# The last expert's rows by blocks, the projections' weights loaded a stage earlier, and their first quad by tiles

## The chip, the cores and the metric

The program runs on one core of one Trainium2 chip. Its time is in device microseconds, the median of several executions. The core has TensorE (PE, with its weight loads as PEld), VectorE (DVE), ScalarE (ACT), GpSimd (POOL), SyncE (SP), which here only issues transfers and waits, and 16 DMA engines that all queues share.

## The reference

Three stages on x of shape 2 x 2048 x 256 (4096 tokens):

```
x = x + 0.5 * ffn(layernorm(x))      # stage 1
x = x + attention(layernorm(x))      # stage 2
x = x + 0.5 * ffn(layernorm(x))      # stage 3, the same weights as stage 1
```

`ffn` is a shared gated network (gelu(x Wsg) * (x Wsu), times Wsd, hidden width 512) plus 16 experts of the same form. Each expert takes the 256 tokens of each of the 2 batches with the highest gate scores, and its rows, times the gate's weight, are added into the output at their tokens (a scatter with addition). `attention` is causal, 16 heads of 16, with rotary positions on queries and keys, and a projection at the end.

## The kernel before

**Blocks.** The program is a row of blocks: constants, `ffn` (stage 1, from line 241, its block opens at L251), `projections` (L1009, block L1019), `exact_shift` (a guarded block that is skipped with these inputs), `attention` (L1444, block L1459), and `ffn` again. Inside a block each engine runs its own instruction list, and semaphores tie the lists together. A block ends for all engines at once: each engine's queue executes a DRAIN, they report to one another, and the next block begins on all of them. The last wait of any engine's list therefore holds the start of the next block.

**Products.** Each float32 product is made of three passes over split operands (`product3`, L168 to L172: high x high, high x low, low x high).

**Experts.** `ffn` works on items of 512 rows: 8 of the shared network, then 16 experts. For an item, TensorE makes the gate and up products (`gu`), ACT and DVE make the hidden rows and their split (`hidden`, `mul`, `low`), TensorE makes the down product (`down`: 4 blocks q of 128 rows, each over 4 chunks c of the hidden width, 3 passes, so 48 matmuls), DVE multiplies it by the gate's weight on the way out of PSUM (`evacuate`, L863, two blocks q after each half h), and GpSimd issues one indirect DMA with addition for each block q (`scatter`, L976). For the last item (`last` in `down`) the chunks that don't need the last hidden rows come first, for q = 0 and 2; then comes the rest of q = 0 and the whole of q = 1, after which `s_D` is signalled for half 0, and then the other half. `scatter` waits for `s_ev`, which DVE signals after both blocks of a half. `pD` holds the four results in two PSUM banks; `pX` and `pC` are two more banks, in which gathered rows are turned, and they are free at that point. At the end GpSimd waits until all scatters have landed:

```
                for k in range(2):
                    s_sc[k].wait(g, E // 2)
```

SyncE loads the experts' weights (`load_weight`, L496). The last one is that of expert 15, after which its list is empty.

**Projections.** This block reads stage 1's result in 8 quads of 4 tiles (512 tokens), in a rotation of 3 buffers `xq`. SyncE issues, in this order: quad 0, `WqkT` (512 KB), `WvT` (256 KB), quad 1, the bias, the rotary table `trig` (2 MB in one), quad 2, and a zero fill of the `shift` rows. For a quad, DVE computes the statistics (L1216, L1223) and the scale, ACT the deviation (L1150) and the normalized rows `xn` (L1156, four instructions, one for each tile), TensorE turns them (L1096, 8 transposes), ACT copies the turned columns (`columns`, L1164), DVE makes their low part (`low_columns`, L1237), and then TensorE makes four row products (`rows`) and `values`. DVE rotates (L1247), GpSimd adds the parts (L1302, L1303, L1307), and SyncE stores the halves (`store`, L1066). From quad 4 on, SyncE also loads heads for the attention (`load_head`, L1435).

The projections' weights are split in this block. ACT's list begins so:

```
                deviation(0)
                a.wait_ge(*s_w.at(2))
                s_wh.done(a.activation(w[0][:, :, :], raw[:, :, :], ACT.Copy))
                normalize(0)
                deviation(1)
                normalize(1)
                columns(0)
```

GpSimd's begins with three small memsets; then it waits for that copy, computes the low part (L1295, a subtraction of 128 x 1536), and sets `sk` (L1296). `rows` waits for this low part (`s_wl`) and for `s_xl`.

## Time and profile before

| what | us |
|---|---|
| runs of the kernel before | 1663.20, 1664.07, 1666.24; median 1664.07 |
| the profiled execution's own time | 1666.25 |
| its span, from the first to the last instruction | 1664.5 |
| time outside the span | 1.75 |

The blocks of the profiled execution, from the span's start: `ffn` up to 499.3, `projections` from 499.33, `attention` from 629.07, the second `ffn` from 1167.78 to the end at 1664.5. Times in the profile are measured from the span's start. In the timeline a row is: start, duration, engine, line, operation, written<-read, shape, count, and in brackets how long the engine sat idle before it and what released it. "POOLq" or "PEq" is that engine's instruction queue, which does waits and drains without being busy. The granted clock of TensorE is 1.0 at 2.4 GHz and 0.5 at 1.2 GHz.

### The profile page before, as it was taken

The page shows a single profiled execution, that of the slowest core. Times are in us where ns is not written, and L with a number is a line of the kernel's source. Part 1 is how long each engine was busy: PE and PEld are TensorE (multiplying, and loading weights), DVE is VectorE, ACT ScalarE, POOL GpSimd, SP SyncE. Part 2 cuts the span into 40 slices and gives each one's busy share as a digit, 9 for nine tenths or more (in the row PEclk, how much of TensorE's full clock was granted, in tenths as well). Part 3 has the DMA queues.
Part 4 walks back from the last instruction along what each step waited for, and adds up shares of the span by engine and source line. Part 5 has one row for each costly group of instructions (what it writes and reads, how often), then busy time and mean ns, then how long its engine had stood idle before and what let it go on. Part 6 is the DMA issues. An engine that isn't in the chain of part 4 may idle for free. (4 is left out here: it accounts for less than half of the span.)

```text
span 1664.5 us, 26482 instructions
## 1 busy us (share of the span) xinstructions
PE 1516.9 (91%) x9945; PEld 1054.1 (63%) x9945; DVE 861.7 (52%) x1848; ACT 995.6 (60%) x1359; POOL 563.2 (34%) x496
## 2 busy tenths in 40 slices
PE   4999999999966867999999999998599999999996
PEld 3788888988955652333333333333478888898895
DVE  6887676766736650032022122122688767676673
ACT  7322255445415757989999999997732225544541
POOL 3000356566445772111121111110300035656644
PEclk9999999999987987999999999999699999999999
DMA  7221256666534799225044343100722126666753
GB/s 274 70 89 51 75 161 152 153 156 152 116 38 168 218 220 198 38 41 77 7 74 80 100 79 65 14 14 29 274 70 89 51 75 161 153 153 155 155 114 38
DMA packets 120752, 183.14 MB, mean 110 GB/s; under 512 B 19568, under 2 KB 83056, under 8 KB 117360
## 3 DMA queue, kind: packets, MB, share of 16 engines
q1 hardware_dynamic: 91440, 130.04, 30.7%
q0 software_dynamic: 29184, 51.40, 14.8%
q8 instruction: 79, 1.29, 0.3%
q14 instruction: 49, 0.40, 0.1%
HBM read 125.82 MB, written 55.57 MB: 109 GB/s over the span
## 5 line engine op out<-in xcount | busy, mean ns | idle before, releaser
L1710 ACT ACTIVATE 8019_pr<-8019_pS 128x1024 f32<-128x1024 f32 x448 | 421.3, 1073 | 17.3 <-PE 8019_pS L1631 16.2
L1661 PE MATMUL 8019_pO<-8019_pr,6201_vres 128*32 128x512 f32 x1792 | 240.2, 608 | 4.5 <-DVE 8019_tO L1735 3.6
L1631 PEld LDWEIGHTS 8019_pS<-sq_rows,sk_rows 50*128 50x128 f32 x896 | 74.9, 186 | 216.9 <-ACT 8019_pr L1710 157.5
L1631 PE MATMUL 8019_pS<-sq_rows,sk_rows 50*128 50x512 f32 x896 | 186.3, 468 | 25.2 <-DMA sq_rows<-shift 20.8
L1735 DVE STREAM_TRANSPOSE 8019_tO<-8019_pO 128x512 f32<-128x512 f32 (+1 forms) x33 | 23.0, 699 | 313.8 <-PE 8019_pO L1661 313.8
L170 PE MATMUL 14694_pGU<-columns_XT,weights_wts 128*128 128x512 f32 x384 | 152.5, 397 | 1.6 <-DVE columns_XT L844 1.6
L170 PE MATMUL 110_pGU<-columns_XT,weights_wts 128*128 128x512 f32 x384 | 152.5, 397 | 1.6 <-DVE columns_XT L844 1.6
L1724 POOL TENSOR_SCALAR_AFFINE_SELECT 8019_pr<-8019_pr 128x512 f32<-128x512 f32 x32 | 21.5, 673 | 381.0 <-ACT 8019_pr L1710 381.0
L171 PE MATMUL 14694_pGU<-columns_XT,weights_wts 128*128 128x512 f32 x384 | 149.8, 390 | 0.0
L171 PE MATMUL 110_pGU<-columns_XT,weights_wts 128*128 128x512 f32 x384 | 149.8, 390 | 0.0
L172 PE MATMUL 110_pGU<-columns_XT,weights_wts 128*128 128x512 f32 x384 | 149.7, 390 | 0.0
L172 PE MATMUL 14694_pGU<-columns_XT,weights_wts 128*128 128x512 f32 x384 | 149.7, 390 | 0.0
L709 ACT ACTIVATE hidden_hT<-110_hf 128x512 fp32r<-128x512 f32 x96 | 60.7, 632 | 144.7 <-DVE 110_hf L834 143.1
L709 ACT ACTIVATE hidden_hT<-14694_hf 128x512 fp32r<-128x512 f32 x96 | 60.7, 632 | 144.3 <-DVE 14694_hf L834 142.8
L976 POOL DMA_INDIRECT out<-14694_eo,14694_idx x64 | 109.6, 1712 | 100.3 <-issue 66.9
L976 POOL DMA_INDIRECT x_after_ffn<-110_eo,110_idx x64 | 109.5, 1711 | 99.9 <-issue 66.6
L170 PE MATMUL 14694_pD<-weights_wts,hidden_hT 128*128 128x256 f32 x384 | 111.0, 289 | 1.4 <-DVE hidden_hT L839 1.4
L170 PE MATMUL 110_pD<-weights_wts,hidden_hT 128*128 128x256 f32 x384 | 111.0, 289 | 1.4 <-DVE hidden_hT L839 1.4
L172 PE MATMUL 110_pD<-weights_wts,hidden_hT 128*128 128x256 f32 x384 | 108.6, 283 | 0.0
L172 PE MATMUL 14694_pD<-weights_wts,hidden_hT 128*128 128x256 f32 x384 | 108.6, 283 | 0.0
L171 PE MATMUL 110_pD<-weights_wts,hidden_hT 128*128 128x256 f32 x384 | 108.5, 283 | 0.0
L171 PE MATMUL 14694_pD<-weights_wts,hidden_hT 128*128 128x256 f32 x384 | 108.5, 283 | 0.0
(318 smaller groups left out, 3334.4 us busy)
## 6 DMA issues: line engine op xcount, KB each, us to landing
token_table<-weights_xn POOLq DMA_DIRECT2D x16, 512.0 KB, 6.3
110_raw_g<-WgT SPq DMA_DIRECT2D x16, 512.0 KB
110_raw_u<-WuT SPq DMA_DIRECT2D x16, 512.0 KB
110_raw_d<-WdT SPq DMA_DIRECT2D x16, 512.0 KB
q_rows<-rows_half SPq DMA_DIRECT2D x32, 256.0 KB, 3.4
k_rows<-rows_half SPq DMA_DIRECT2D x32, 256.0 KB, 3.3
sq_rows<-q_rows SPq DMA_DIRECT2D x32, 256.0 KB
sk_rows<-k_rows SPq DMA_DIRECT2D x32, 256.0 KB
```

Of the source, the lines that this page charges most:

```text
L170: pe.matmul(out, w_hi, x_hi, start=start, stop=False)
L171: pe.matmul(out, w_hi, x_lo, start=False, stop=False)
L172: return pe.matmul(out, w_lo, x_hi, start=False, stop=stop)
L709: s_hh.done(a.activation(hT[0][:, i % 2, f, :], hf[:, f % 2, :], ACT.Copy))
L976: s_sc[k].part(g.indirect_dma_start(out, bass.IndirectOffsetOnAxis(rows_[:, q:q + 1], 0), eo[:, k, q, :], None, compute_op=ALU.add), 16)
L1631: m = t_.matmul(to[:, e, :], key, query, start=True, stop=True)
L1661: m = t_.matmul(pO[e * 32:(e + 1) * 32, off:off + wd], vres[:, (g // GB) * TPB + kt, at:at + 32], from_(e), start=n == first[j], stop=n == ...
L1710: s_exp.done(a.activation(to, pS[:, u % RING, :, :], ACT.Exp, scale=HD ** -0.5))
L1724: s_mask.done(g.affine_select(out=blk_, in_=blk_, compare_op=ALU.is_ge, fill=0.0, base=0, pattern=[[0, GH], [1, P]], channel_multiplier=-1))
L1735: s_copy.done(v.transpose(tO[:, part], pO[:, part]))
```

## The change

- **The last expert, in both `ffn` blocks.** Each block q of the down product gets a PSUM bank of its own (`own_bank`: two halves of `pD`, `pX` and `pC`). The early chunks are those of q = 0 and 1. After each block's last chunk TensorE signals `s_Dq`; DVE evacuates that block alone and signals `s_evq`; GpSimd scatters it after that signal.
- **The wait for the scatters' landing** moves from the end of GpSimd's list to the end of SyncE's.
- **Loads of the projections' weights** move into the first `ffn` block: SyncE issues both behind the last expert's weights, into a buffer at a fixed address (`qkv_raw`) that nothing else uses in that block.
- **Splitting these weights**: the high part moves from ACT (Copy) to GpSimd (`tensor_copy`), behind its three small memsets and in front of the subtraction.
- **The first quad** is loaded by four DMAs of one tile (128 KB), each with its own semaphore. DVE's statistics start tile by tile; ACT signals each normalized tile (`s_n0`), and TensorE turns tile by tile. ACT now does `columns(0)` ahead of `normalize(1)`.
- **The rotary table** is loaded in four parts of 512 KB, with quads 1 and 2 ahead of parts 0 and 1; SyncE's order is: four tiles, bias, quad 1, part 0, quad 2, parts 1, 2, 3, zero fill.

```diff
+            s_Dq, s_evq = sig("pe_last_D"), sig("dve_last_ev")
+            own_bank = lambda q: (pD[:, 0, 0, :], pX[:, 0:D], pD[:, 1, 0, :], pC[:, 0:D])[q]
...
+                if following:
+                    following(sp)
+                for k in range(2):
+                    s_sc[k].wait(sp, E // 2)
...
+                def rows_down(d, q, c, to):
+                    k = slot(d)
+                    rows_ = slice(q * P, (q + 1) * P)
+                    return self.product3(t_, to, hT[0][:, d % 2, c, rows_], hT[1][:, d % 2, c, rows_],
+                                         weight(k, 2, 0)[:, c, :], weight(k, 2, 1)[:, c, :], c == 0, c == FC - 1)
...
-                    s_ev.wait(t_, 2 * (d - 1) + (2 if last else h + 1))
-                    order = [(q, c) for q in (2 * h, 2 * h + 1) for c in range(FC) if (q, c) not in early]
-                    if h == 0:
-                        order = early + order
-                    for q, c in order:
-                        if last and (q, c) == (0, FC - 1):
-                            t_.wait_ge(*s_hl.at(4 * (d + 1)))
...
+                def last_down(d):
+                    t_.wait_ge(*s_hl.at(4 * d + FC - 1))
+                    s_wl.wait(t_, 3 * (d - J) + 3)
+                    s_ev.wait(t_, 2 * d)
+                    for q in range(2):
+                        for c in range(FC - 1):
+                            rows_down(d, q, c, own_bank(q))
+                    t_.wait_ge(*s_hl.at(4 * (d + 1)))
+                    for q in range(4):
+                        for c in range(FC - 1 if q < 2 else 0, FC):
+                            m = rows_down(d, q, c, own_bank(q))
+                        s_Dq.done(m)
...
+                    if s > NI:
+                        last_down(NI - 1)
+                    elif s > J + 1:
...
+                def evacuate_last(d):
+                    k = d % 2
+                    s_sc[k].wait(v, (d - J) // 2)
+                    s_wt.wait(v, d - J + 1)
+                    for q in range(4):
+                        v.wait_ge(*s_Dq.at(q + 1))
+                        s_evq.done(v.tensor_scalar(eo[:, k, q, :], own_bank(q), wt[:, k, q:q + 1], 0.5,
+                                                   ALU.mult, ALU.mult))
...
-                        if q % 2 == 0:
+                        if item == NI - 1:
+                            g.wait_ge(*s_evq.at(q + 1))
+                            self.settle(g)
+                        elif q % 2 == 0:
                             g.wait_ge(*s_ev.at(2 * item + q // 2 + 1))
                             self.settle(g)
...
                         scatter(s - 2)
-                for k in range(2):
-                    s_sc[k].wait(g, E // 2)
...
-                load(0)
-                s_w.done(sp.dma_start(raw[:, :, 0:2 * D], self.ins["WqkT"].rearrange("(c p) f -> p c f", p=P)))
-                s_w.done(sp.dma_start(raw[:, :, 2 * D:], self.ins["WvT"].rearrange("(c p) f -> p c f", p=P)))
-                load(1)
+                for j in range(4):
+                    s_x0[j].done(sp.dma_start(xq[:, 0, j, :], xv[0][:, j, :]))
                 s_c.done(sp.dma_start(bias[:, :], self.ins["b_rows"]))
-                s_c.done(sp.dma_start(trig[:, :, :], self.ins["c_rope"]))
-                load(2)
+                for k in range(S // W):
+                    if k < 2:
+                        load(k + 1)
+                    part = slice(k * W, (k + 1) * W)
+                    s_trig[k].done(sp.dma_start(trig[:, :, part], self.ins["c_rope"][:, :, part]))
                 sp.wait_ge(*s_clear.at(1))
                 s_zero.done(sp.dma_start(self.shift.rearrange("h c (k s) -> h (c k) s", s=512),
                                          zero[:, :].unsqueeze(1).to_broadcast([B * H, 2 * S // 512, 512])))
...
-                turn(0)
+                for j in range(4):
+                    t_.wait_ge(*(s_n0.at(j + 1) if j < 3 else s_xn.at(1)))
+                    for c in range(DC):
+                        m = t_.transpose(pX[:, c, j * P:(j + 1) * P], xn[:, 0, j, c * P:(c + 1) * P], self.ident[:, :])
+                        if j == 3:
+                            s_T.done(m)
...
+                        if q == 0 and j < 3:
+                            s_n0.done(m)
                     s_xn.done(m)
...
                 deviation(0)
-                a.wait_ge(*s_w.at(2))
-                s_wh.done(a.activation(w[0][:, :, :], raw[:, :, :], ACT.Copy))
                 normalize(0)
                 deviation(1)
+                columns(0)
                 normalize(1)
-                columns(0)
...
-                    s_x[q % 3].wait(v, q // 3 + 1)
+                    if q > 0:
+                        s_x[q % 3].wait(v, q // 3 + (q % 3 > 0))
                     s_mv.wait(v, q - 1)
                     for j in range(4):
+                        if q == 0:
+                            v.wait_ge(*s_x0[j].at(1))
                         m = v.bn_stats(st6[:, q % 2, j, :], xq[:, q % 3, j, :])
...
-                    v.wait_ge(*s_c.at(2))
+                    v.wait_ge(*s_c.at(1))
+                    if n < 4 * (S // W):
+                        v.wait_ge(*s_trig[q].at(1))
...
+                g.wait_ge(*s_w.at(0))
+                s_wh.done(g.tensor_copy(w[0][:, :, :], raw[:, :, :]))
                 g.wait_ge(*s_wh.at(1))
                 s_wl.done(g.tensor_tensor(w[1][:, :, :], raw[:, :, :], w[0][:, :, :].bitcast(f32), ALU.subtract))
                 s_clear.done(g.memset(self.sk[:, 0, :, :].bitcast(f32), 1.0))
...
+    def load_projection_weights(self, sp):
+
+        s_w = self.counter("proj_w", 16)
+        s_w.done(sp.dma_start(self.qkv_raw[:, :, 0:2 * D], self.ins["WqkT"].rearrange("(c p) f -> p c f", p=P)))
+        s_w.done(sp.dma_start(self.qkv_raw[:, :, 2 * D:], self.ins["WvT"].rearrange("(c p) f -> p c f", p=P)))
...
-        prog.ffn(ins["x"], prog.x1, first=EARLY)
+        prog.ffn(ins["x"], prog.x1, first=EARLY, following=prog.load_projection_weights)
```

## Rows read from the trace of the kernel before

**Rows 1.** The page, part 1: busy time and share of the span of each engine.
```profile
PE 1516.9 (91%) x9945; PEld 1054.1 (63%) x9945; DVE 861.7 (52%) x1848; ACT 995.6 (60%) x1359; POOL 563.2 (34%) x496
```

**Rows 2.** Windows: stretch, length, busy time by engine, granted clock, DMA share, GB/s.
```profile
499.30:520.00 20.70, 7.19 (x21) 5.60 (x22) 8.28 (x26) 8.94 (x15) 8.75 (x5) 0.50 0.74 266
595.00:615.50 20.50, 16.00 (x96) 12.87 (x94) 12.44 (x21) 11.66 (x21) 18.98 (x12) 1.00 1.01 189
```

**Rows 3.** Timeline of the end of the second ffn: down product, evacuation, scatter.
```profile
1645.43 0.38 PE L170 MATMUL 14694_pD<-weights_wts,hidden_hT 128*128 128x256 f32 x1 [1.44 <-DVE hidden_hT L839]
...
1649.78 0.88 DVE L863 TENSOR_SCALAR 14694_eo<-14694_pD,14694_wt 128x256 f32<-128x256 f32 x2 [3.62 <-PE 14694_pD L172]
...
1651.44 1.55 POOL L976 DMA_INDIRECT out<-14694_eo,14694_idx  x1 [6.85 <-DVE 14694_eo L863]
...
1657.02 1.56 POOL L976 DMA_INDIRECT out<-14694_eo,14694_idx  x1 [0.30 <-issue]
```

**Rows 4.** Timeline of the first ffn's end, POOL alone.
```profile
491.86 1.55 POOL L976 DMA_INDIRECT x_after_ffn<-110_eo,110_idx  x1 [0.30 <-issue]
499.33 0.52 POOL L1290 MEMSET 6206_zero<- 32x512 f32 x1 [5.92 <-POOLq L251]
```

**Rows 5.** Queue instructions by line: count, duration ns min/median/max, first and last start.
```profile
L59 POOLq EVENT_SEMAPHORE  x1: 17/17/17, 495.7 to 495.7; - x1
L251 POOLq DRAIN  x2: 3168/3170/3172, 495.9 to 1661.1; - x2
```

**Rows 6.** Attention's end, where SyncE has the last wait: store, its landing, next load.
```profile
1163.43 0.36 SPq L1574 DMA_DIRECT2D x_after_attn<-rows_acc  x1
1167.78 0.36 SPq L492 DMA_DIRECT2D hidden_xq<-x_after_attn  x1
...
x_after_attn<-rows_acc SPq DMA_DIRECT2D x1, 512.0 KB, 3.9
```

**Rows 7.** Timeline of the projections' first 21 us.
```profile
500.26 0.94 POOL L1293 MEMSET 6201_vres<- 128x512 f32 x1
500.80 0.47 SPq L1057 DMA_DIRECT2D 6206_xq<-x_after_ffn  x1
503.09 1.41 DVE L1216 BATCH_NORM_STATS2 6206_st<-6206_xq 128x6 f32<-128x256 f32 x4 [3.29 <-DMA 6206_xq<-x_after_ffn]
505.60 0.16 DVE L1231 SCALAR_TENSOR_TENSOR 6206_shift<-6206_mv,6206_rstd 128x4 f32<-128x4 f32 x1
505.75 1.48 ACT L1188 ACTIVATE 6206_w<-6206_raw 128x1536 fp32r<-128x1536 f32 x1 [0.40 <-DMA 6206_raw<-WvT]
507.10 1.41 DVE L1216 BATCH_NORM_STATS2 6206_st<-6206_xq 128x6 f32<-128x256 f32 x4 [1.34 <-DMA 6206_xq<-x_after_ffn]
507.14 2.06 ACT L1156 ACTIVATE 6206_xn<-6206_xq,6206_shift,6206_rstd 128x256 f32<-128x256 f32 x4
507.32 3.43 POOL L1295 TENSOR_TENSOR 6206_w<-6206_raw,6206_w 128x1536 fp32r<-128x1536 f32 x1 [6.11 <-ACT 6206_w L1188]
509.10 0.28 ACT L1150 ACTIVATE 6206_std<-6206_mv,49_eps 128x4 f32<-128x4 f32 x1
509.25 1.97 PE L1096 MATMUL 6206_pX<-49_ident,6206_xn 128*128 128x128 f32 x8 [22.96 <-ACT 6206_xn L1156]
512.78 1.05 ACT L1164 ACTIVATE sk_xT<-6206_pX 128x512 fp32r<-128x512 f32 x2
514.78 0.77 PE L170 MATMUL 6206_pQ<-sk_xT,6206_w 128*128 128x512 f32 x1 [3.56 <-issue]
519.99 1.03 PE L1096 MATMUL 6206_pX<-49_ident,6206_xn 128*128 128x128 f32 x8
```

**Rows 8.** Landing of SyncE's stores of 256 KB (L1066), us from issue: min, median, max.
```profile
DMA to landing us min/median/max: 2.8/3.4/13.3
```

**Rows 9.** SyncE's last load before the change's new ones.
```profile
441.62 0.37 SPq L496 DMA_DIRECT2D 110_raw_d<-WdT  x1
```

**Rows 10.** Timeline of the projections' end.
```profile
620.70 1.06 ACT L1175 ACTIVATE rows_half<-sq_turns 128x1024 fp32r<-128x1024 f32 x1 [9.10 <-DMA q_rows<-rows_half]
```

More of the change, by code:

```diff
@@ L28 @@
 EARLY = 2
+QKV_AT = 216 * 1024
 NBITS = 30
@@ L197, in load_constants @@
         self.x_at = at
+        self.qkv_raw = nc.alloc_sbuf_tensor_at("qkv_raw", [P, DC, 3 * D], self.f32, offset=QKV_AT)
         with self.scope() as t, nc.Block() as blk:
@@ L238, in _, with ffn @@
                 dve.wait_ge(s_cast, 3)
-    def ffn(self, x, out, first=0):
+    def ffn(self, x, out, first=0, following=None):
         nc, ALU, ACT, AX, bass = self.nc, self.ALU, self.ACT, self.AX, self.bass
@@ L938, in _ @@
                         split(s, 1)
-                    if s > J + 1:
+                    if s > NI:
+                        evacuate_last(NI - 1)
+                    elif s > J + 1:
                         evacuate(s, 0)
```

32 lines of the change are left out of this document (16 added, 16 removed).

## Prediction

> **What bounds the kernel now.** The page shows TensorE busy for 91% of the span [rows 1], so most of the kernel is TensorE's pace, and this change leaves that work as it is. It acts in three places where TensorE stands still. The windows show two of them around the projections: in their first 21 us TensorE is busy for 7.2 us at granted clock 0.50, which is its 1.2 GHz level, and from 595 on the DMA engines are full, at share 1.01 [rows 2]. The timeline of an `ffn` block's end shows the third: the last down product starts at 1645.43, the first scatter at 1651.44, and scatters follow 1.86 us apart ((1657.02 - 1651.44) / 3) until 1658.58 [rows 3]. After that nothing is computed until the span's end at 1664.5. The first `ffn` block ends in the same way: last scatter done at 493.41, next block at 499.33 [rows 4]. The queue view names what fills those 5.92 us: the landing is seen at 495.7, and then GpSimd's DRAIN runs from 495.9 for 3.17 us, the same length in both blocks, on an idle engine [rows 5].
>
> **Part 1: the last rows by blocks.** Before, DVE's first evacuation waits for 33 of the 48 matmuls, and the first scatter for two evacuations. From the first matmul to DVE's start are 4.35 us for the 33 [rows 3], 0.13 each at most; the tail behind the last one is in it, so I take 0.12. Afterwards block 0 is complete after 21 matmuls (18 early, 3 more): 12 fewer, 1.4 us. Its evacuation alone takes about 0.44 of the pair's 0.88: 0.4 us. The first scatter starts **1.8 us earlier**, near 1649.6. Later blocks are ready in time: each comes 12 matmuls (1.4 us) after the one before, and the scatters are 1.86 apart. Of that spacing 0.30 is issue [rows 3], also where a wait stands in between, so I count nothing for two more waits on GpSimd. The matmuls are the same 48. The early ones (18 x 0.12 = 2.2 us, as many as now) cover the wait for the last hidden rows as before.
>
> **Part 2: who awaits the landing.** Once GpSimd doesn't wait, its DRAIN can start right behind the last scatter, say 0.1 us, instead of 2.5 us (493.41 to 495.9 [rows 4, 5]). If its 3.17 us is a fixed length, it ends 3.3 us behind the scatter. SyncE sees the landing 2.3 us behind it (495.7 - 493.41) and ends the block faster: the attention block's last store, issued at 1163.43, lands 3.9 us later at 1167.3, and the next block's load starts at 1167.78 [rows 6], 0.45 us later. So SyncE would be ready at 2.8 us, and the drain decides. From the drain's end to the next block took 0.26 us (495.92 + 3.17 = 499.09 to 499.33 [rows 4, 5]). Scatter to next block is then 0.1 + 3.17 + 0.25 = 3.5 us instead of 5.92: **2.4 us**. The trace doesn't show this drain with transfers in flight. Its bounds: if it starts to count only at the landing, the gain is about 0.2 us; if it is nearly free behind the scatter, SyncE decides and the gain is 3.1. I take the fixed length, since both blocks show 3.17 within 4 ns [rows 5]. Each `ffn` block's end is worth 1.8 + 2.4 = 4.2 us, twice: **8.4 us**. Queued behind SyncE's new wait is nothing but the block's end. Ahead of it stand the two new weight loads.
>
> **Part 3: the projections' first quad** (times from the block's start at 499.33). Now row products start at 514.78, so at 15.45 [rows 7]. The chain: quad 0 lands at 3.75, statistics until 5.17, scale and shift until 6.43; then ACT copies the weights (505.75 to 507.23), normalizes, waits for quad 1's shift, normalizes that, and only at 512.78 copies quad 0's columns [rows 7].
>
> Afterwards:
> - *Tiles.* Four issues instead of one. The fourth goes out at the place that 500.80 had: 1.47 [rows 7]. A landing takes 2.8 us at the least, for 256 KB [rows 8], and 3.7 for the present quad (503.09 - 499.33 [rows 7]). I take 2.8, the nearer in size: it lands at 4.3, its statistics (one of four, 0.4) end at 4.7 against 5.17. The bounds are +0.4 and -0.5 us.
> - *ACT.* From statistics to shift 1.26 us (504.50 to 505.76 [rows 7]), and no copy behind it: 6.0. Four tiles 2.06: 8.1. TensorE turns three of them meanwhile and the last in 0.5 (a quarter of 1.97, plus a start): 8.65.
> - *Quad 1.* ACT's next deviation needs its statistics. Its DMA is sixth in SyncE's queue, so issued at about 2.5, landed at 6.2 (3.7 us); from landing to deviation are 2.0 us (507.10 to 509.10) and 0.28 for it [rows 7]: 8.5. That is just hidden behind the turns. If it took 6.3 us, as it did behind the weights (500.80 to 507.10 [rows 7]), columns would start at 11.1.
> - *Columns to products.* 512.78 to 514.78 is 2.0 us [rows 7]: products at 10.75.
> - *GpSimd's copy* isn't in the trace. Nearest are ACT's 1.48 us for the same tile and GpSimd's subtraction, 3.43 with two inputs [rows 7]. It starts at 1.87 (501.20). Copy and subtraction end at 6.8 to 8.75. The products need them at 10.75, so 2 us cover even the upper bound; I take 2.3 for it. Without the cover it would cost what it overruns.
>
> **Gain 15.45 - 10.75 = 4.7 us**, bounds 2.3 (late quad 1) and 5.1. The table's parts: part 0 is behind 1 MB, needed at about 13; the old 2 MB in one came behind 1.75 MB and held nobody.
>
> The Trainium skill speaks against four small loads: "DMA: Bandwidth & Descriptors", section "Anatomy of one DMA — SWDGE (gpsimd) path", gives each DMA about 2.0 us fixed and then the bytes at 436 GB/s. By this, for a path that isn't SyncE's, a quad is an estimated 3.2 us and a tile 2.3; the last tile would land at 3.8 and gain about 0.5 us rather than my 0.4, if the fixed parts overlap. The trace has 3.75 for the quad, so it is a little slower than the rule.
>
> **Does the 4.7 us last?** The window at 595 has GpSimd busy 18.98 of 20.5 us and the DMA engines at 1.01 [rows 2], and ACT waits 9.10 us for a store's landing [rows 10]. A DMA-bound tail can swallow a head start. But all these transfers are issued by SyncE behind stores that wait for GpSimd, so the queue begins to fill earlier too. I count the whole.
>
> **Part 4: the moved loads.** 768 KB go out behind 441.62 [rows 9], 58 us before they are needed, with no expert left to load. The last expert's own transfer is ahead in the same queue. At the rate of 266 GB/s that the projections' start shows [rows 2] they are 3 us of traffic beside scatters, for whose landing only the next item's scatters wait. The first blocks' items go on at TensorE's pace; I cost it at nothing. Without that cover it would be those 3 us.
>
> **The clock.** TensorE starts the quad at the low level either way: eight transposes take 1.97 us then and 1.03 when the clock is up [rows 7]. It was up at 519.99, 5.2 us after the products began [rows 7]. A shifted start may meet an earlier or later rise: plus or minus 1 us.
>
> **Sum.** 8.4 + 4.7 = 13.1 us. Of the profiled execution's 1666.25 us (span 1664.5 and 1.75 outside) that leaves 1653.1. This execution was 2.2 us above the median, so from 1664.07: **1651.0 us**.
>
> **Rivals.**
> - *The drain follows the landing.* GpSimd's drain may need its transfers finished before its 3.17 us begin. For it: in both blocks it came right behind the landing, so the trace can't separate the two. Against: no reason in its constant length. Each end loses 2.2 us: 1651.0 + 4.4 = 1655.4.
> - *The head start is lost in part.* Quad 1 comes late (1653.4), or the DMA-bound tail takes all of it (1655.7). For: [rows 2, 10]. Against: the queue's order.
> - *Both together*: 1658 to 1660.
> - *The loads' fixed costs add up* instead of overlapping: about 5.5 us later for the last tile, no gain in the projections, 1655.7. Against: stores issued 0.6 us apart landed in 2.8 us each at best [rows 8].
> - *The change does little*: its waits are only renamed, within 3 us of before. Part 1's 1.8 us twice already speak against it.
> - *Slower: the clock stays down in the projections.* The quad's work by tiles leaves TensorE's starts more scattered. Low clock makes its work take about twice as long [rows 7], so each us at it costs about 0.5 us of work. It would eat the 13 us only from 26 us more at the low level on; 40 us more would give 1651 + 20 = 1671. Against: it was up after 5.2 us, and at 1.00 in the busy window at 595 [rows 2].
>
> **Chances.** Forecast 0.58 (its own range 1648.5 to 1653); drain follows landing 0.17; head start lost in part or whole, for any of the three causes, 0.15; both 0.05; does little 0.03; slower by the clock 0.02. The range runs from 1648, for a cheap drain (0.7 us at each end) and a good rise of the clock, to 1656.5, for either single loss; that leaves out about 0.15. A measurement of this kernel tells 0.2% (3.3 us) from no change. Faster by more than that: 0.95; within it 0.03; slower 0.02.
>
> **What would show it.** Right: the last expert's first scatter 4.2 us behind its first down product instead of 6.0; GpSimd's drain right behind the last scatter, 3.2 us long; next block 3.5 us behind the scatter; projections' products 10.5 to 11 us into their block, with quad 1 landed by 6.5; attention's start as much earlier as these. Wrong: a drain of 5 us or more; a second idle stretch of ACT ahead of the columns; products waiting for GpSimd's copy; stores at the projections' end landing at the old times.

## The result and the profile after

| | before | after |
|---|---|---|
| median of 5 runs, us | 1664.69 (1663.20 to 1666.24) | 1655.38 (1650.51 to 1656.72) |
| the profiled execution, us | 1666.25, span 1664.5 | 1650.51, span 1648.7 |

The ratio is 0.9923, 95% interval 0.9903 to 0.9942, so 9.7 to 16.1 us less; the medians alone are 9.3 us apart. A second measurement of the same kernel (below) gave 0.9914, 0.9887 to 0.9942. The forecast of 13.1 us less lies inside both intervals. The median of 1655.38 is inside the forecast's range, but 4.4 above its 1651.0 and at the numbers of two rivals, 1655.4 and 1655.7; the second measurement's 1652.41 is not. So the times alone don't choose between them, and the traces have to. The profiled execution is 15.7 us shorter, and its blocks say where. Worked out from the first instruction of each block:

| us | before | after | gain |
|---|---|---|---|
| first `ffn`, from the span's start | 499.34 | 495.27 | 4.07 |
| projections with the skipped block | 129.74 | 121.93 | 7.81 |
| of that, up to the first row product | 15.44 | 11.41 | 4.03 |
| attention | 538.70 | 538.58 | 0.12 |
| second `ffn`, to the span's end | 496.76 | 492.88 | 3.88 |

Page, part 1, and windows of the kernel after, as in [rows 1, 2] (the windows are moved with the block):

```profile
PE 1508.1 (91%) x9943; PEld 1047.6 (64%) x9945; DVE 862.7 (52%) x1848; ACT 994.2 (60%) x1358; POOL 564.2 (34%) x497
```

```profile
495.27:516.00 20.73, 11.48 (x53) 9.13 (x54) 12.85 (x38) 9.52 (x18) 12.60 (x8) 0.65 0.70 229
591.00:611.50 20.50, 8.67 (x51) 6.63 (x51) 7.77 (x14) 8.34 (x16) 15.57 (x10) 0.85 1.06 260
```

In the first 21 us of the projections TensorE is busy for 11.5 us instead of 7.2, and for part of them at the high clock. The second window is later in the block's work than [rows 2] shows, since the block is ahead; the DMA engines are as full.

Timeline of the end of the second `ffn`, kernel after, PE, DVE and POOL, as in [rows 3]:

```profile
1633.81 0.38 PE L171 MATMUL 14727_pD<-weights_wts,hidden_hT 128*128 128x256 f32 x1 [1.44 <-DVE hidden_hT L859]
...
1636.72 0.48 DVE L892 TENSOR_SCALAR 14727_eo<-14727_pD,14727_wt 128x256 f32<-128x256 f32 x1 [2.18 <-PE 14727_pD L173]
...
1637.99 1.55 POOL L1010 DMA_INDIRECT out<-14727_eo,14727_idx  x1 [5.02 <-DVE 14727_eo L892]
...
1643.57 1.56 POOL L1010 DMA_INDIRECT out<-14727_eo,14727_idx  x1 [0.30 <-issue]
```

The first scatter starts 4.18 us behind the last down product's start, before 6.01. The scatters stand 1.86 apart as before, with 0.30 of issue between them: each block's rows are there in time.

Queue instructions of that line, kernel after (durations in ns, first and last start), and POOL's next instruction, as in [rows 4, 5]:

```profile
L253 POOLq DRAIN  x2: 7515/7524/7532, 487.5 to 1640.9; - x2
```

```profile
490.15 1.55 POOL L1010 DMA_INDIRECT x_after_ffn<-111_eo,111_idx  x1 [0.30 <-issue]
495.27 0.51 POOL L1336 MEMSET 6213_zero<- 32x512 f32 x1 [3.57 <-POOLq L253]
```

The DRAIN now enters the queue while the scatters run, so its 7.5 us are mostly their time. It ends at 495.02, 3.32 us behind the last scatter (491.70) and 1.03 us behind the landing (493.99), and the next block begins at 495.27: 3.57 us instead of 5.92.

Timeline of the projections' start, kernel after, as in [rows 7]:

```profile
497.01 1.45 POOL L1341 CAST 6213_w<-qkv_raw 128x1536 fp32r<-128x1536 f32 x1
497.30 1.97 DVE L1260 BATCH_NORM_STATS2 6213_st<-6213_xq 128x6 f32<-128x256 f32 x4 [1.56 <-DMA 6213_xq<-x_after_ffn]
498.55 3.41 POOL L1343 TENSOR_TENSOR 6213_w<-qkv_raw,6213_w 128x1536 fp32r<-128x1536 f32 x1
500.37 1.62 DVE L1275 SCALAR_TENSOR_TENSOR 6213_shift<-6213_mv,6213_rstd 128x4 f32<-128x4 f32 x1
501.91 1.39 DVE L1260 BATCH_NORM_STATS2 6213_st<-6213_xq 128x6 f32<-128x256 f32 x4
502.02 2.07 ACT L1197 ACTIVATE 6213_xn<-6213_xq,6213_shift,6213_rstd 128x256 f32<-128x256 f32 x4 [1.90 <-DVE 6213_shift L1275]
504.00 0.28 ACT L1191 ACTIVATE 6213_std<-6213_mv,49_eps 128x4 f32<-128x4 f32 x1
504.53 0.16 DVE L1275 SCALAR_TENSOR_TENSOR 6213_shift<-6213_mv,6213_rstd 128x4 f32<-128x4 f32 x1
504.66 1.09 ACT L1207 ACTIVATE sk_xT<-6213_pX 128x512 fp32r<-128x512 f32 x2 [0.38 <-PE 6213_pX L1168]
506.68 0.77 PE L171 MATMUL 6213_pQ<-sk_xT,6213_w 128*128 128x512 f32 x1 [1.84 <-issue]
510.90 1.03 PE L1132 MATMUL 6213_pX<-49_ident,6213_xn 128*128 128x128 f32 x8
```

The row to look at is 500.37: DVE's shift of 128 x 4 elements takes 1.62 us. The same instruction on the next quad takes 0.16. It ends at 501.99, and GpSimd's subtraction ends at 501.96. The kernel before has it too, and the prediction passed over it: its second shift started under the same subtraction (507.32 to 510.75 in [rows 7]) and lasted until 510.77:

```profile
509.63 1.14 DVE L1231 SCALAR_TENSOR_TENSOR 6206_shift<-6206_mv,6206_rstd 128x4 f32<-128x4 f32 x1
```

### The profile page after: what moved, and what is told of

The parts are those of the page before. It is cut to its first block and busy times, and to the rows that moved or that the text cites. A ratio compares the mean times of both kernels' runs of the same rounds, so it can differ in the third digit from the quotient of the medians.

```text
span 1648.7 us, 26498 instructions
## 1 busy us (share of the span) xinstructions
PE 1508.1 (91%) x9943; PEld 1047.6 (64%) x9945; DVE 862.7 (52%) x1848; ACT 994.2 (60%) x1358; POOL 564.2 (34%) x497
## 3 DMA queue, kind: packets, MB, share of 16 engines
q8 instruction: 79, 1.29, 0.3%
## 5 line engine op out<-in xcount | busy, mean ns | idle before, releaser
L1764 ACT ACTIVATE 8052_pr<-8052_pS 128x1024 f32<-128x1024 f32 x448 | 421.2, 1073 | 17.2 <-PE 8052_pS L1685 15.9
L1715 PE MATMUL 8052_pO<-8052_pr,6208_vres 128*32 128x512 f32 x1792 | 240.3, 606 | 5.9 <-DVE 8052_tO L1789 3.7
L1685 PEld LDWEIGHTS 8052_pS<-sq_rows,sk_rows 50*128 50x128 f32 x896 | 74.5, 185 | 213.9 <-ACT 8052_pr L1764 153.8
L1685 PE MATMUL 8052_pS<-sq_rows,sk_rows 50*128 50x512 f32 x896 | 185.3, 466 | 24.1 <-DMA sq_rows<-shift 19.6
L171 PE MATMUL 111_pGU<-columns_XT,weights_wts 128*128 128x512 f32 x384 | 152.5, 397 | 1.6 <-DVE columns_XT L864 1.6
L171 PE MATMUL 14727_pGU<-columns_XT,weights_wts 128*128 128x512 f32 x384 | 152.5, 397 | 1.6 <-DVE columns_XT L864 1.6
L172 PE MATMUL 14727_pGU<-columns_XT,weights_wts 128*128 128x512 f32 x384 | 149.8, 390 | 0.0
L172 PE MATMUL 111_pGU<-columns_XT,weights_wts 128*128 128x512 f32 x384 | 149.8, 390 | 0.0
L173 PE MATMUL 111_pGU<-columns_XT,weights_wts 128*128 128x512 f32 x384 | 149.8, 390 | 0.0
L173 PE MATMUL 14727_pGU<-columns_XT,weights_wts 128*128 128x512 f32 x384 | 149.8, 390 | 0.0
L1010 POOL DMA_INDIRECT out<-14727_eo,14727_idx x64 | 109.6, 1712 | 98.5 <-issue 67.0
L1010 POOL DMA_INDIRECT x_after_ffn<-111_eo,111_idx x64 | 109.5, 1711 | 98.1 <-issue 66.6
L171 PE MATMUL 111_pD<-weights_wts,hidden_hT 128*128 128x256 f32 x376 | 108.7, 289 | 1.4 <-DVE hidden_hT L859 1.4
L171 PE MATMUL 14727_pD<-weights_wts,hidden_hT 128*128 128x256 f32 x376 | 108.7, 289 | 1.4 <-DVE hidden_hT L859 1.4
L173 PE MATMUL 14727_pD<-weights_wts,hidden_hT 128*128 128x256 f32 x376 | 106.3, 283 | 0.0
L173 PE MATMUL 111_pD<-weights_wts,hidden_hT 128*128 128x256 f32 x376 | 106.3, 283 | 0.0
L172 PE MATMUL 14727_pD<-weights_wts,hidden_hT 128*128 128x256 f32 x376 | 106.2, 283 | 0.0
L172 PE MATMUL 111_pD<-weights_wts,hidden_hT 128*128 128x256 f32 x376 | 106.2, 283 | 0.0
```

The costliest lines, as they stand in the source:

```text
L171: pe.matmul(out, w_hi, x_hi, start=start, stop=False)
L172: pe.matmul(out, w_hi, x_lo, start=False, stop=False)
L173: return pe.matmul(out, w_lo, x_hi, start=False, stop=stop)
L1010: s_sc[k].part(g.indirect_dma_start(out, bass.IndirectOffsetOnAxis(rows_[:, q:q + 1], 0), eo[:, k, q, :], None, compute_op=ALU.add), 16)
L1685: m = t_.matmul(to[:, e, :], key, query, start=True, stop=True)
L1715: m = t_.matmul(pO[e * 32:(e + 1) * 32, off:off + wd], vres[:, (g // GB) * TPB + kt, at:at + 32], from_(e), start=n == first[j], stop=n == ...
```

## Experiments

The theory after the result: the last expert's rows by blocks and SyncE's wait bring 4 us at each `ffn` end, in the size worked out; the projections bring 4.0, less than the 4.7 of the forecast because the subtraction holds VectorE; what the profiled execution has beyond that goes with TensorE's granted clock. "First product" below is counted from the block's start, "rest of the block" is the projections' length minus it.

### The three parts alone

`e1_blocks`: the kernel before with the last item by blocks, landing still awaited by GpSimd.

```diff
-                    if s > J + 1:
+                    if s > NI:
+                        last_down(NI - 1)
+                    elif s > J + 1:
...
                 for k in range(2):
                     s_sc[k].wait(g, E // 2)
```

> The kernel before with the last expert's rows evacuated and scattered by blocks, and nothing else; GpSimd still awaits the landing. Theory (the parts are separate terms): the first of the last scatters starts 1.8 us earlier in each ffn block, the drain still starts behind the landing and takes 3.17 us, so 5.9 us lie between the last scatter and the next block; 3.6 us faster than before in all. Rival (blocks only help together with the moved wait): less than 1 us.

Measured: 1662.19 us median of 12 runs against 1667.49 of 23, ratio 0.9971 (0.9955 to 0.9988), so 2.0 to 7.5 us less. In its trace the first scatter comes 4.17 and 4.19 us behind the last down product's start, and the next block still 5.83 behind the last scatter (5.86 at the end). It does 1.83 us at each end and nothing else there; the 3.6 lie in the interval.

`e2_sync_waits`: the kernel before with the wait on SyncE.

```diff
-                for k in range(2):
-                    s_sc[k].wait(g, E // 2)
...
                 for e in range(2, E):
                     for w in range(3):
                         load_weight(e, w)
+                for k in range(2):
+                    s_sc[k].wait(sp, E // 2)
```

> The kernel before with the wait for the scatters' landing at the end of SyncE's list instead of GpSimd's, and nothing else. Theory (GpSimd's drain ends about 3.3 us behind its last scatter, whether the transfers have landed or not): last scatter to next block 3.5 us instead of 5.9, 4.8 us faster in all. Rival (the drain needs the landing, and the changed kernel's trace shows something else): 5.7 us from scatter to next block, within 0.5 us of before.

Measured: 1660.55 us (6 runs), ratio 0.9952 (0.9934 to 0.9969), so 8.0 us less, between 5.2 and 11.0. Its trace, queue instructions and then POOL's timeline:

```profile
L251 POOLq DRAIN  x2: 8496/8500/8503, 488.7 to 1652.2; - x2
```

```profile
492.40 1.55 POOL L978 DMA_INDIRECT x_after_ffn<-110_eo,110_idx  x1 [0.30 <-issue]
497.49 0.52 POOL L1290 MEMSET 6206_zero<- 32x512 f32 x1 [3.54 <-POOLq L251]
```

3.54 and 3.52 us instead of 5.92 and 5.95: 4.8 us in all, as expected. The interval begins just above that. Where the rest of the 8.0 comes from isn't shown. The clock (below) could give it: in this kernel's profiled execution the projections, which the edit leaves alone, take 125.64 us instead of 129.74, with no fall of the clock in them. But its attention is 3.2 us longer, and one trace doesn't split a median.

`e3_projections`: the kernel before with only the change's projections and weight loads; its first scatter (6.00, 6.02) and its block ends (5.96, 5.83) are those of before.

```diff
-        prog.ffn(ins["x"], prog.x1, first=EARLY)
+        prog.ffn(ins["x"], prog.x1, first=EARLY, following=prog.load_projection_weights)
```

> The kernel before with only the projections' part of the change: moved loads, weights split on GpSimd, first quad by tiles, table in parts. Theory (head start of 4.0 us in the first quad, the rest of the projections' 7.8 us in the changed kernel's profile is TensorE's granted clock): row products start 11.4 us into the block, the block takes 125.7 us if the clock falls inside it as before and near 122 us if it doesn't; the median 4 to 6 us faster. Rival (the change itself speeds the later quads): the block takes 122 us whatever the clock does, the median 7.8 us faster.

Measured: 1666.17 us (12 runs), ratio 0.9986 (0.9969 to 1.0003), so between 5.2 less and 0.5 more. The median of 4 to 6 us less that was expected didn't come, and the times alone don't show this part. The trace is sharper than the times: first product 11.41 us into the block, against 15.44, and the block 125.53 long against 129.74, 4.2 less. The rest of the block is 114.12 against 114.30: the head start goes through to the attention whole.

### What holds the projections' first quad

`e4_split_first`: GpSimd splits the weights ahead of its three memsets, so that the subtraction ends before VectorE's shift is due.

```diff
-                s_clear.done(g.memset(zero[:, :], 0.0))
-                g.memset(self.vres[:, :, H * VW:], 0.0)
...
                 g.wait_ge(*s_w.at(0))
                 s_wh.done(g.tensor_copy(w[0][:, :, :], raw[:, :, :]))
                 g.wait_ge(*s_wh.at(1))
                 s_wl.done(g.tensor_tensor(w[1][:, :, :], raw[:, :, :], w[0][:, :, :].bitcast(f32), ALU.subtract))
+                s_clear.done(g.memset(zero[:, :], 0.0))
+                g.memset(self.vres[:, :, H * VW:], 0.0)
```

> The changed kernel with GpSimd's weight split ahead of its three small memsets. Theory (GpSimd's two-input subtraction holds up VectorE's small two-input instruction that makes quad 0's shift: 1.62 us instead of 0.16, 500.37 to 501.99, and it ends when the subtraction ends): the subtraction ends 1.8 us earlier, at about 5.0 us into the block, the shift takes 0.16 us, products start 1.4 us earlier, at 10.0 us; about 1.4 us faster than the changed kernel. Rival (the shift's long duration has nothing to do with GpSimd): it stays at 1.6 us and products stay at 11.4.

Measured: first product at 10.39, 1.02 us earlier than after where 1.4 were expected; ratio 0.9932 (0.9913 to 0.9951), 1657.40 us (6 runs), in which no gain over the kernel after shows. Timeline, DVE and POOL:

```profile
498.29 3.41 POOL L1339 TENSOR_TENSOR 6213_w<-qkv_raw,6213_w 128x1536 fp32r<-128x1536 f32 x1
501.89 0.16 DVE L1275 SCALAR_TENSOR_TENSOR 6213_shift<-6213_mv,6213_rstd 128x4 f32<-128x4 f32 x1
```

With the subtraction ended at 501.70 the shift takes 0.16 us. Nothing else on VectorE was changed: the hold is the subtraction's. After it the next limit shows: ACT's deviation of quad 1 (504.90 to 505.20) holds the columns, which start at 505.11.

`e5_one_load`: the changed kernel with quad 0 in one load of 512 KB.

```diff
-                for j in range(4):
-                    s_x0[j].done(sp.dma_start(xq[:, 0, j, :], xv[0][:, j, :]))
+                s_x0[0].done(sp.dma_start(xq[:, 0, :, :], xv[0]))
```

> The changed kernel with quad 0 in one DMA of 512 KB instead of four of 128 KB; everything else, also the transposes by tile, stays. Theory (the shift waits for GpSimd's subtraction, which ends at 6.7 us into the block whatever the load does): the statistics end at 5.2 us instead of 4.0, and the first product stays at 11.4 us, so the four loads bring nothing in this version. Rival (loads by tile carry through): products 1.0 us later, at 12.4 us.

Measured, one execution (1651.87 us): the statistics end 1.1 us later (5.10 us into the block, 4.0 after), and the first product comes at 11.41, where it came before. Timeline:

```profile
499.74 3.41 POOL L1342 TENSOR_TENSOR 6213_w<-qkv_raw,6213_w 128x1536 fp32r<-128x1536 f32 x1
...
502.66 0.52 DVE L1274 SCALAR_TENSOR_TENSOR 6213_shift<-6213_mv,6213_rstd 128x4 f32<-128x4 f32 x1
```

The shift starts later and is held less; it ends with the subtraction (503.15) either way. So in the changed kernel the four loads bring nothing up to the first product.

`e6_high_on_act`: the weights' high part back on ACT, behind the first deviation.

```diff
                 deviation(0)
+                a.wait_ge(*s_w.at(0))
+                s_wh.done(a.activation(w[0][:, :, :], raw[:, :, :], ACT.Copy))
                 normalize(0)
...
-                g.wait_ge(*s_w.at(0))
-                s_wh.done(g.tensor_copy(w[0][:, :, :], raw[:, :, :]))
```

> The changed kernel with the weights' high part made by ScalarE ahead of the first normalized tile, as before, and GpSimd's subtraction behind it; the loads stay a stage earlier. Theory (the copy costs its 1.48 us on ScalarE, but the subtraction then comes too late to hold up quad 0's shift and holds up quad 1's instead): shift of quad 0 0.16 us long, first product within 0.5 us of the changed kernel's 11.4. Rival (moving the copy off ScalarE is the gain): products 1.5 us later, at 12.9 us.

Measured, one execution (1653.65 us): first product at 11.06, 0.35 us earlier than after. ACT spends 1.47 us on the copy ahead of normalizing, but the subtraction starts later, so the first shift takes 0.16 us, and the hold falls on the second quad's shift. That one stands ahead of the first quad's low columns in DVE's list: they start 0.93 us behind ACT's columns instead of 0.63, so only 0.3 us of this hold reaches the product.

```profile
503.75 0.16 DVE L1277 SCALAR_TENSOR_TENSOR 6213_shift<-6213_mv,6213_rstd 128x4 f32<-128x4 f32 x1
...
507.44 0.98 DVE L1277 SCALAR_TENSOR_TENSOR 6213_shift<-6213_mv,6213_rstd 128x4 f32<-128x4 f32 x1
```

`e7_columns_late`: the changed kernel with `normalize(1)` ahead of `columns(0)`, as before.

```diff
-                columns(0)
                 normalize(1)
+                columns(0)
```

> The changed kernel with ScalarE's first columns behind the normalizing of quad 1, as they stood before the change; the other edits stay. It prices the order of the two by itself. Quad 1's normalizing is ready at about 9.8 us into the block and takes 2.1 us, so the columns start at about 12 instead of 9.4 and the first product comes 14.0 us into the block instead of 11.4: 2.6 of the 4.0 us of head start are the order's. Rival: the columns were held by TensorE's turns or by quad 1 anyway, and the product moves by under 1 us.

Measured, one execution (1663.40 us): first product at 13.84, 2.4 us later. Of the 4.0 us of head start the order of two calls on ACT is worth 2.4; 1.6 are left for everything else in that part. This execution is 12.9 us longer than the profiled one of after. The projections have 4.8 of it; the rest lies in the `ffn` blocks and the attention, where nothing was edited.

### What the run-to-run spread is

`after_again`: the changed kernel once more, beside the following runs.

> The changed kernel once more, for the profile and for a comparison on one chip with the next one. Theory (its profile at 1650.5 us was one without falls of the granted clock inside the projections and the attention; the projections' block is 110.5 us behind the first product without such falls and 114.3 with two of them): first product at 11.4 us into the block, the drains' ends 3.3 us behind the last scatter, and the projections' block at 121.9 us without falls, 125.7 with two. Rival (the block's length varies by something else): a length that doesn't go with the number of falls.

Measured: 1652.41 us (1647.23 to 1658.63, 6 runs) against 1668.34 (11 runs). The time goes with TensorE's mean granted clock: the shortest run, 1647.23, has 0.975, the longest, 1658.63, has 0.966. Over the projections the traces show what differs. Windows of `e4_split_first` around a pause of TensorE that begins 36 us behind the first product, and of the kernel after at the same place:

```profile
543.50:545.50 2.00, 0.07 (x1) 0.00 (x0) 2.00 (x4) 1.93 (x4) 0.54 (x1) 1.00 0.97 324
545.50:548.90 3.40, 3.25 (x9) 1.96 (x10) 1.29 (x2) 3.40 (x10) 3.40 (x3) 0.50 0.83 243
548.90:557.00 8.10, 8.10 (x52) 7.09 (x50) 6.57 (x17) 4.09 (x8) 5.82 (x4) 1.00 0.40 129
```

```profile
542.60:544.70 2.10, 0.07 (x2) 0.08 (x4) 2.10 (x4) 2.03 (x4) 0.77 (x1) 1.00 0.96 338
544.70:548.10 3.40, 3.40 (x21) 2.51 (x22) 2.30 (x4) 3.40 (x9) 3.40 (x3) 1.00 0.75 218
```

Both stand still for about 2 us, since the norms wait for ACT's squares. Behind the pause one execution gets the 1.2 GHz level for 3.4 us and issues 9 matmuls in them, the other keeps 2.4 GHz and issues 21. Pauses of 1.4 to 2.1 us begin some 36 and 73 us behind the first product in thirteen of the fourteen profiled executions. Behind the first the clock fell in five of them and behind the second in seven; in the kernel before behind both, in the two profiled executions of the changed kernel behind neither. But it fell behind neither in `e1_blocks` and `e2_sync_waits` too, whose projections are those of before. A third pause of 2.0 us, at 60, never had a fall. For the first pause the traces show what goes with a fall: where it begins 31.6 to 32.2 us behind the moment at which the clock last rose, the clock fell (five executions), and where it begins 32.3 to 32.9 us behind it, it didn't (eight). No such order shows for the second pause, and no run moved a pause on purpose. The rest of the block is 110.3 to 110.9 us with no fall (six executions), 111.4 and 112.4 with one, 112.9 to 114.6 with two. So one fall goes with 0.6 to 2.1 us and two with 2.0 to 4.3. Of the 7.8 us that the projections became shorter, 3.8 lie behind the first product: they go with the two falls that the profiled execution of before has and that of after has not, and an estimated 1 us of them with the clock's rise, which comes 3.0 us behind the first product instead of 5.1. The 23 runs of before beside the first experiments have a mean clock of 0.9657, the 11 runs of the changed kernel 0.9710. Part of this is the change itself: the low stretch around the start of the projections lasts 20.5 us instead of 30.7, and most of what it lost was standing still. How much the change has to do with the falls stays open.

### Could it be faster still?

`e8_columns_first`: `e4_split_first`, and on ACT `columns(0)` ahead of `deviation(1)`.

```diff
-                deviation(1)
                 columns(0)
+                deviation(1)
```

> The changed kernel with GpSimd's split ahead of its memsets and ScalarE's quad-0 columns ahead of its deviation of quad 1. Theory (with the shift freed, ScalarE's columns wait for the deviation of quad 1, whose load is the sixth): columns start right behind the last transposes and products 0.3 us earlier than with the split alone, at 10.1 us; 1.3 us faster than the changed kernel. Rival (the columns wait for the transposes anyway): 10.4 us.

Measured: 1654.47 us, ratio 0.9925 (0.9900 to 0.9950); first product at 10.88, later than the 10.39 it was to improve. The columns did start earlier (7.90 us into the block, 8.39 before), but DVE's list has the scale of quad 1 ahead of the low columns of quad 0, and that scale waits for the deviation just moved back. The wait had only changed its engine.

`e11_low_first`: the same, and on DVE `low_columns(0)` ahead of `scale(1)`.

```diff
-                scale(1)
                 low_columns(0)
+                scale(1)
```

> The split first and the columns first, as in the earlier run, and in VectorE's list the first quad's low columns ahead of the second quad's scale. By the theory that the low columns were held only by their place in VectorE's list (it waited there for the second quad's deviation), the first product comes 10.0 to 10.1 us into the projections, against 10.88 there and 11.4 in the changed kernel: some 1.3 us less than the changed kernel, a median ratio to the kernel before about 0.991. Rival: quad 1 is late anyway; its normalizing, now behind the columns, keeps TensorE waiting at the second turn and the product's head start is given back by the block's end (length of the block minus the first product's time over 111 us with no fall of the clock inside).

Measured: 1653.41 us (6 runs), ratio 0.9910 (0.9885 to 0.9934); first product at 10.15. Timeline:

```profile
503.32 1.08 ACT L1207 ACTIVATE sk_xT<-6213_pX 128x512 fp32r<-128x512 f32 x2 [0.56 <-PE 6213_pX L1168]
503.95 1.29 DVE L1281 TENSOR_TENSOR sk_xT<-6213_pX,sk_xT 128x512 fp32r<-128x512 f32 x2 [0.51 <-ACT sk_xT L1207]
504.30 0.30 ACT L1191 ACTIVATE 6213_std<-6213_mv,49_eps 128x4 f32<-128x4 f32 x1
505.35 0.76 PE L171 MATMUL 6213_pQ<-sk_xT,6213_w 128*128 128x512 f32 x1 [1.84 <-issue]
```

The low columns follow the columns at once. The rest of the block is 113.4 us with two falls of the clock in this execution, inside what two falls give elsewhere, so quad 1's later normalizing costs nothing that shows.

`e12_norms_later`: the same, and TensorE's norms one row product later.

```diff
                     rows(4 * q)
+                    rows(4 * q + 1)
                     if q >= 1:
                         norms(q - 1)
-                    rows(4 * q + 1)
```

> As the kernel above, and TensorE's norms of a quad one row product later. In the changed kernel TensorE waits 11.0 us in all in the projections ahead of these norms, for ScalarE's squares, 1.35 us each time. Theory: the squares are there 1.4 us later, so the waits go and with them most of the pauses behind which the granted clock fell in some executions: block length minus first product 101 to 104 us, no fall of the clock in the projections, 6 to 9 us less in all than the kernel above. Rival: another engine paces the block (GpSimd is busy for 18.3 of 20 us at 520 to 540, DVE and ACT for 13 to 16), the same wait appears a few products later, and the block's length stays within 2 us of the kernel above.

Measured: 1650.62 us (6 runs), ratio 0.9909 (0.9884 to 0.9933). Groups by line, PE alone, from 512 to 617 us (busy, mean ns, idle before and its releaser), first of `e11_low_first` and then of this one:

```profile
L1132 PE MATMUL 6213_pX<-49_ident,6213_xn 128*128 128x128 f32 x48 | 6.2, 272 | 0.0
L1162 PE MATMUL 6213_pN<-6213_squares,6213_head_of 128*32 128x512 bf16 x32 | 5.8, 443 | 11.2 <-ACT 6213_squares L1213 11.2
```

```profile
L1132 PE MATMUL 6213_pX<-49_ident,6213_xn 128*128 128x128 f32 x48 | 6.6, 279 | 7.7 <-ACT 6213_xn L1197 7.7
L1162 PE MATMUL 6213_pN<-6213_squares,6213_head_of 128*32 128x512 bf16 x32 | 4.9, 384 | 1.0 <-ACT 6213_squares L1213 1.0
```

The expected 101 to 104 us behind the first product didn't come, and the rival holds: 10.2 us of waiting for the squares are gone, and 7.7 us of waiting for ACT's normalized rows stand before the turns, with 2.5 before the row products. ACT's list paces TensorE here, whichever of its results is asked for first. The first product comes at 9.91, and the rest of the block is 111.43 with no fall, no better than after's 110.52; the clock rose 5.0 us behind the first product instead of 3.0, which by halves is an estimated 1 us. What did change is the form of the pauses: none is over 1.35 us now, and the clock did not fall in the profiled execution.

The changed kernel (0.9914), `e11_low_first` (0.9910) and `e12_norms_later` (0.9909) can't be told apart by time; the 1.3 us of the first product is below the spread.

### What the 3.3 us behind the last scatter are

`e9_op_behind`: a memset of 128 x 1 on GpSimd behind the last scatter.

```diff
                     if s > J + 1:
                         scatter(s - 2)
+                g.memset(mx[:, 0:1], 0.0)
```

> The changed kernel with one small memset on GpSimd behind the last scatter. It asks what the 3.3 us between the last scatter and the end of GpSimd's drain are. If the drain waits for the time that the last indirect DMA's descriptors take, counted from the scatter, the end of the drain stays 3.3 us behind the scatter. If it is a fixed time behind the last instruction of GpSimd, or comes only where a DMA was the last, it moves: 0.2 us later or as short as on an engine without a DMA.

Measured, one execution (1653.16 us): the drain ends at 496.37, 3.30 us behind the last scatter (493.07), as in the kernel after. So it is not short merely because another instruction comes last. In the projections block of the kernel after, which issues no indirect DMA, GpSimd's DRAIN ends 0.07 us behind its last instruction (612.43 to 612.50). The memset ran inside the scatter's time and ended 0.12 us behind it, too close for this run to tell whether the 3.3 us count from the scatter or from the last instruction.

The kept traces tell that they count from neither. In eleven of the profiled executions SyncE awaits the landing. Four of their 22 `ffn` ends, us behind the end of the last scatter:

| execution, end | last landing | end of the drain |
|---|---|---|
| `e8_columns_first`, first | 2.16 | 3.20 |
| `after_again`, second | 2.20 | 3.23 |
| the kernel after, first | 2.29 | 3.32 |
| `e6_high_on_act`, first | 2.33 | 3.37 |

The drain's end moves with the landing. In the 20 ends of the ten without the memset it lies 3.20 to 3.37 us behind the scatter, but always 1.034 to 1.036 us behind the landing (1.08 and 1.06 with the memset). The scatter's first packet starts 1.29 to 1.30 us ahead of the scatter's end in the ends above, so a later landing isn't a later start. The drain does wait for its transfers, and about 1.03 us of it are left then. No run moved the landing on purpose, so this is read from the traces and not tested by an edit. Where GpSimd itself awaits the landing (`before`, `e1_blocks`, `e3_projections`) the drain takes 3.17 us and ends 3.43 behind it. Why only 1.03 are left when it entered the queue before isn't shown.

## Why the prediction was right, and where its sizes were off

**Part 1, 1.8 us at each end.** Right: 6.00 to 4.16 and 6.01 to 4.18, and later scatters kept their 1.86. (Block 1 is complete 3 matmuls behind block 0 and not 12, DVE starts on it 0.40 us later; that changes nothing, since the scatters are slower.)

**Part 2, 2.4 us at each end.** The size was right, the reason was not. The next block comes 3.57 us behind the scatter and the span's end 3.52, forecast 3.5. But the drain isn't a fixed 3.17 us behind the scatter: its end follows the landing by 1.03 us, as the last experiment's table shows. So the rival was right that the drain needs its transfers finished, and wrong that the whole 3.17 us come behind them (that would have been 5.7 us). The forecast's 0.1 + 3.17 and the measured 2.29 + 1.03 give the same 3.3 us; that they do is luck. The sign that was named, a drain right behind the last scatter and 3.2 us long, didn't come either: the DRAIN starts ahead of the last two scatters and is 7.5 us long, which by the forecast's "5 us or more" would have meant wrong. Both parts together gained 4.19 and 4.26 us from the last down product to the next block or the end, for the forecast's 4.2; the whole blocks became 4.07 and 3.88 shorter.

**Part 3, 4.7 us.** The mechanism was right and the size 0.7 too high. Two terms were off, and they nearly cancel. The last tile was to land at 4.3 and its statistics to end at 4.7; they landed at 3.55 and ended at 4.0. The nearest row, a store of 256 KB with 2.8 us at the least [rows 8], was too long for a load of 128 KB, whose first took 2.0; the 3.8 that the prediction set beside its 4.3 was nearer. Then "from statistics to shift 1.26 us": it took 2.7, as the subtraction held the shift for 1.46. Normalizing, turning and the 2.0 us from columns to products went as worked out. The sum is 10.75 - 0.7 + 1.46, less 0.1: 11.4. The 0.1 is a slip in the forecast, whose 8.65 + 2.0 is 10.65. So the products missed the 10.5 to 11 us that were named as a sign. The step that failed is that GpSimd's copy and subtraction were costed by when their result is needed ("2 us cover even the upper bound"). That cover was real: the copy took 1.46 us for the 2.3 I took, and the result was there at 6.7. What they cost was VectorE's time, as a row of the kernel before would have told, the second shift of 1.14 us beside the 0.16 of the first [rows 7].

The Trainium skill has the rule, "SBUF — State Buffer", section "Who interferes with whom": a VectorE instruction with two inputs in SBUF contends with a GpSimd instruction that reads SBUF; the ports that they share are an exclusive lock, and the order of issue decides which of the two is blocked. The traces agree: each shift that starts under the subtraction is held to its end (1.62, 1.14, 0.52 and 0.98 us in the rows above, 1.60 in `e3_projections` and 1.52 in `e7_columns_late`), and the others take 0.16 us. GpSimd's memsets, which read nothing, held none: the quad-1 shift at 504.53 ran under the one of 3.51 us.

**"Does the 4.7 us last?"** Yes: of the 4.0 us that there were, all. At the same number of falls of the clock the rest of the block is as long with the new projections as with the old: with two 112.9 to 114.6 in four kernels (114.12 in `e3_projections`) against 114.30, with none 110.52 and 110.29 for the changed kernel against 110.83 for `e1_blocks` and 110.33 for `e2_sync_waits`. This holds although the DMA engines are full at its end and ACT still waits 8.11 us for a store's landing, [rows 10] 9.10. The attention is 0.12 us shorter. The rival of a swallowed head start is out.

**Part 4, the moved loads at nothing.** Right. SyncE issued them at 442.17 and 442.96. From its load of the last expert's weights to the start of the last scatter are 50.24 us in the kernel before and 50.24 in `e3_projections`, which has the moved loads and the old end. In the kernel after they are 48.39, shorter by what the blocks gained. The first `ffn` as a whole became shorter by 4.07 of the 4.19 us that its end gained; the missing 0.1 lies ahead of these loads (441.76 against 441.62).

**The clock, plus or minus 1 us.** The shifted start itself was inside this. In the kernel after the granted clock is 0.50 up to 509.7, 3.0 us and 7 products behind the first one, and 1.00 from there; before, it was 0.50 for 5.1 us and 12 products (514.78 to 519.9). The high level came 2.1 us earlier, an estimated 1 us of gain. What the prediction did not look for are the falls further on, behind pauses of 2 us: with the earlier rise they go with 3.8 us between the two profiled executions. The time goes with the clock between runs of one kernel too, which differ by 9 to 14 us within each series of 11 to 23 runs. That the medians came out 9.3 us apart once and 15.9 the other time, around a change that the traces put at 12 (7.95 by the two `ffn` blocks and 4.03 up to the first product), fits this; the split of the medians was only argued.

## What to carry to other kernels

An engine with slack still costs: an instruction moved to GpSimd is to be costed by what it blocks on VectorE too, and the trace shows this as one short instruction with two lengths. The wait at the block's end did better on SyncE, whose own DRAIN takes 7 ns, because GpSimd's long one could then begin before the landing. When a wait is moved to another engine's list, read what stands behind it in every list, since `e8_columns_first` and `e12_norms_later` only passed the wait on. A change of a few microseconds is better read from the distance between two events in the trace than from times that spread by ten.

## What was unexpected in the hardware

- GpSimd's drain at the end of an `ffn` block takes 3.17 us if GpSimd has awaited the landing of its indirect DMAs itself. If it enters the queue before, it ends 1.034 to 1.036 us behind the last landing (20 ends), 3.20 to 3.37 behind the last scatter. In the projections block of the kernel after, where none was issued, it ends 0.07 us behind GpSimd's last instruction.
- A VectorE instruction on 128 x 4 elements took up to 1.62 us instead of 0.16, until GpSimd's subtraction ended.
- GpSimd's copy of 128 x 1536 with conversion takes 1.46 us, as ACT's does (1.48), and its subtraction of two inputs of the same size 3.41.
- Behind the same 2 us pause of TensorE the granted clock fell in some executions, for 3.4 us each time, and not in others. At the first such pause the falls came only where it began up to 32.2 us behind the clock's last rise; what decides it at the second stays open.
